# Gated two-layer block on one core: a new order in SP's DMA queue, gate and up products over three PSUM banks, and VectorE taking each unit one slot later

## What is computed

```
x = x + tanh(g_xattn[0]) * _L0_xattn_ref(_layernorm(x, axis=-1), ctx_1024, L0_xattn_W, L0_xattn_b)
x = x + tanh(g_ffn[0]) * _L0_ffn_ref(_layernorm(x, axis=-1), L0_ffn_w_up, L0_ffn_w_down)
x = x + tanh(g_xattn[1]) * _L1_xattn_ref(_layernorm(x, axis=-1), ctx_1024, mask, Wq, bq, Wkv, bkv, Wout, bout, 16)
x = x + tanh(g_ffn[1]) * _L1_ffn_ref(_layernorm(x, axis=-1), gate_w, up_w, down_w, s_in, s_in_down)
```

```
gate_out = nvfp4_linear(x, gate_w, s_in[0])
up_out = nvfp4_linear(x, up_w, s_in[0])
hidden = jax.nn.silu(gate_out) * up_out
return nvfp4_linear(hidden, down_w, s_in_down[0])
```

## Time and profile before

| | |
|---|---|
| median of 3 runs | 1825.38 us (1817.82 to 1830.28) |
| profiled execution | 1823.66 us, span of its trace 1821.9 us |
| mean granted TensorE clock | 0.892 of 2.4 GHz |
| busy share: PE, DVE, ACT, POOL | 75%, 78%, 38%, 13% |
| chain that ended last | issue 43%, DVE 26%, PE 18%, DMA 4%, SP's queue 4%, ACT 3% |

### The profile page before, as it was taken

The page is one execution under the profiler, slowest core; times in us unless marked ns, Lnnn a source line. Parts: engine busy times, 40 slices in busy tenths (PEclk is TensorE's granted clock), DMA queues, the critical chain, the costliest instruction groups (busy, mean ns, idle before and its releaser), DMA issues.

```text
span 1821.9 us, 24307 instructions
## 1 busy us (share of the span) xinstructions
PE 1371.2 (75%) x8120; PEld 705.4 (39%) x8120; DVE 1421.6 (78%) x2437; ACT 692.5 (38%) x2105; POOL 243.9 (13%) x197
## 2 busy tenths in 40 slices
PE   5044737799787978698778978797869886988663
PEld 4021315344453436344543345343634453434321
DVE  6988896878787687787787878768777778786695
ACT  2112206451455227441644146422734164425310
POOL 1102200131003200230013100320013001310000
PEclk9556868899889989999999989998999999999888
DMA  9175761042101420233004210142023300420012
GB/s 348 68 243 146 188 143 36 6 88 64 42 1 35 93 59 14 35 62 77 25 7 87 58 48 1 35 93 59 14 35 65 75 24 6 87 58 24 7 24 51
DMA packets 267433, 120.08 MB, mean 66 GB/s; under 512 B 244090, under 2 KB 244602, under 8 KB 265750
## 3 DMA queue, kind: packets, MB, share of 16 engines
q1 hardware_dynamic: 267286, 118.27, 26.5%
HBM read 49.04 MB, written 8.39 MB: 32 GB/s over the span
## 4 chain that ended last, share of the span: by engine, by line
issue 43%; DVE 26%; PE 18%; DMA 4%; SPq 4%; ACT 3%; POOL 2%; POOLq 0%; DVEq 0%; ACTq 0%
PE bank L1075 13%; PE bank L1164 5%; DVE amax L826 2%; DVE pair L835 2%; DVE hid L831 2%; SPq L314 2%; DVE th L868 2%; SPq L303 1%; DVE pair L850 1%; DMA region<-region 1%; ACT region L535 1%; DVE pair L843 1%; DMA hqt<-pair 1%; DVE sc L797 1%; DVE stats L686 1%
## 5 line engine op out<-in xcount | busy, mean ns | idle before, releaser
L1164 PE MATMUL bank<-w_dn,region 128*128 128x512 fp8e4 x1024 | 243.7, 386 | 40.0 <-DMA region<-region 40.0
L1075 PE MATMUL bank<-w_up,xt 128*128 128x512 fp8e4 x1024 | 248.6, 391 | 32.7 <-ACT region L499 17.4
L1075 PE MATMUL bank<-w_gate,xqt 128*128 128x512 bf16 x512 | 147.9, 416 | 122.2 <-DVE th L868 78.4
L508 ACT ACTIVATE th<-bank,half_cg 128x512 f32<-128x512 f32 x128 | 88.0, 687 | 350.2 <-PE bank L1075 350.2
L426 POOL TENSOR_TENSOR region<-g,region 128x512 f16<-128x512 f32 x128 | 178.9, 1402 | 300.9 <-ACT region L499 292.9
L868 DVE SCALAR_TENSOR_TENSOR th<-th,bank 128x512 f32<-128x512 f32 x128 | 87.6, 684 | 138.4 <-ACT th L508 138.3
L535 ACT ACTIVATE region<-bank,nm 128x77 f32<-128x77 f32 x512 | 160.0, 345 | 68.2 <-DVE nm L914 68.2
L1075 PE MATMUL bank<-w_down,hqt 128*128 128x512 bf16 x512 | 134.3, 422 | 56.9 <-DMA hqt<-pair 56.9
L496 ACT ACTIVATE g<-bank 128x512 f32<-128x512 f32 x128 | 76.4, 597 | 247.2 <-PE bank L1075 188.2
L1164 PEld LDWEIGHTS bank<-w_dn,region 128*128 128x128 f16 x1024 | 101.0, 99 | 167.4 <-issue 52.0
L1075 PEld LDWEIGHTS bank<-w_up,xt 128*128 128x128 f16 x1024 | 102.0, 101 | 163.5 <-issue 55.4
(11 more groups left out here) (206 smaller groups left out, 2473.6 us busy)
## 6 DMA issues: line engine op xcount, KB each, us to landing
xin<-in_x SPq DMA_DIRECT2D x16, 512.0 KB, 4.1
out_x<-x SPq DMA_DIRECT2D x16, 512.0 KB, 3.0
region<-in_w_up_t SPq DMA_DIRECT2D x1, 4096.0 KB, 12.9
hid<-in_gate_w SPq DMA_DIRECT2D x4, 1024.0 KB, 5.2
x<-in_gate_w SPq DMA_DIRECT2D x4, 1024.0 KB, 6.1
hid<-in_up_w SPq DMA_DIRECT2D x4, 1024.0 KB, 5.2
x<-in_up_w SPq DMA_DIRECT2D x4, 1024.0 KB, 5.8
hid<-in_down_w SPq DMA_DIRECT2D x4, 1024.0 KB, 4.9
```

Of the source, the lines that this page charges most:

```text
L508: eng.activation(th[:, u % 2, :], bank[4][:, :], ACT.Tanh, scale=half_cg[:, :]).then_inc(sg["th"], 1)
L1075: last = mm(out, lhs, rhs, start=(n == 0), stop=(n == len(pairs) - 1))
L1164: last = mm(bank[2 + t % 2][:, :], ht[i][:, t % 2, f, :], w_dn[:, f, :], start=(f == 0 and i == 0), stop=(f == KF - 1 and i == 1))
```

## The change

There are three edits.

1. `gu_bank(u, i)` deals the products of the units over banks 4, 5 and 6 in turn, in place of bank 4 for every gate and bank 5 for every up. A gate product now waits for hid of unit u-2, and an up product for hg of unit u-1. Unit 1's gate is the first to use bank 6, which phase A uses too, and so waits for `p3l`. ScalarE and VectorE read the banks by the same rule.
2. In phase B VectorE takes `hidden` of a unit in the slot behind TensorE's, and `QUANT_AT` moves by one slot: parts 0 to 2 to `TILE_AT`+5, parts 3 and 4 to `TILE_AT`+6. `POST_AT`, and with it the slots of down4 and out4, stays. In the tail VectorE's order is as it was.
3. SP's `turns` issues the transposes of hidden tiles 0 and 1 of stage 2 ahead of the first `turn_h`, and those of tiles 2 and 3 ahead of the second.

```diff
-QUANT_AT = {TILE_AT[t] + 4 + i: (t, q) for t in range(TILES) for i, q in enumerate(((0, 1, 2), (3, 4)))}
+QUANT_AT = {TILE_AT[t] + 5 + i: (t, q) for t in range(TILES) for i, q in enumerate(((0, 1, 2), (3, 4)))}
...
+        def gu_bank(u, i):
+
+            return 4 + (2 * u + i) % 3
...
                 if g1 is not None:
                     turn_ht(g1, 0)
+                    turn_ht(g1, 1)
                 turn_h(g, 0)
                 if g1 is not None:
-                    turn_ht(g1, 1)
                     turn_ht(g1, 2)
+                    turn_ht(g1, 3)
                 turn_h(g, 1)
-                if g1 is not None:
-                    turn_ht(g1, 3)
                 store(g, 0)
...
-                        if s in GU_AT:
-                            hidden(s4, GU_AT[s])
+                        if s - 1 in GU_AT:
+                            hidden(s4, GU_AT[s - 1])
...
-                for i, (w, read) in enumerate(((w_gate, "hg"), (w_gup, "hid"))):
-                    if u:
-                        want(pe, read, g, u)
+                for i, w in enumerate((w_gate, w_gup)):
+                    if i == 0 and u >= 2:
+                        want(pe, "hid", g, u - 1)
+                    if i == 1 and u:
+                        want(pe, "hg", g, u)
...
+                    if u == 1 and i == 0:
+                        want(pe, "p3l", g)
-                    last = product(bank[4 + i][:, :], [(xqt[:, t, k, :], w[:, k, ns]) for k in range(KD)])
+                    last = product(bank[gu_bank(u, i)][:, :], [(xqt[:, t, k, :], w[:, k, ns]) for k in range(KD)])
```

More of the change, by code:

```diff
@@ L507, in tanh4 @@
                     want(act, "hid", g, u - 1)
-                eng.activation(th[:, u % 2, :], bank[4][:, :], ACT.Tanh, scale=half_cg[:, :]).then_inc(sg["th"], 1)
+                eng.activation(th[:, u % 2, :], bank[gu_bank(u, 0)][:, :], ACT.Tanh, scale=half_cg[:, :]).then_inc(sg["th"], 1)
             def query(g, c):
@@ L867, in hidden @@
                 want(dve, "th", g, u + 1)
-                eng.scalar_tensor_tensor(th[:, u % 2, :], th[:, u % 2, :], 1.0, bank[4][:, :], ALU.add,
+                eng.scalar_tensor_tensor(th[:, u % 2, :], th[:, u % 2, :], 1.0, bank[gu_bank(u, 0)][:, :], ALU.add,
                                          ALU.mult).then_inc(sg["hg"], 1)
@@ L871, in hidden @@
                 want(dve, "gu", g, u + 1)
-                eng.tensor_tensor(buf[:, n * D:(n + 1) * D], th[:, u % 2, :], bank[5][:, :], ALU.mult).then_inc(sg["hid"], 1)
+                eng.tensor_tensor(buf[:, n * D:(n + 1) * D], th[:, u % 2, :], bank[gu_bank(u, 1)][:, :], ALU.mult).then_inc(sg["hid"], 1)
             def quant4(g, t, parts, buf=hid):
```

## The result

| | before | after |
|---|---|---|
| median | 1821.6 us (4 runs) | 1898.16 us (4 runs, 1892.76 to 1898.78) |
| ratio, 95% interval | | 1.0408 [1.037, 1.0446] |
| profiled execution, its span | 1823.66, 1821.9 us | 1898.78, 1897.0 us |
| mean granted TensorE clock | 0.892 | 0.868 of 2.4 GHz |
| down4 of tile 3 waits, in each of six phases | 4.21 to 4.86 us | 14.21 to 14.25 us |

The kernel is 4.1% slower, or 76.6 us. 1887 was forecast, with 1871 to 1902 as the range. A fourth run of the kernel before brought its median from 1825.38 to 1821.6 us.

A forecast was written before the change was run, and what follows sets the result against it. The prediction took VectorE and TensorE handing work to each other as the bound, with down4 of tile 3 waiting on VectorE's rounding. 60.0 (loop) + 3.8 (seventh phase) - 1.8 (tail) = +62.0 us gave 1887 us, range 1871 to 1902.

The forecast's parts named there:

- What bounds the kernel: VectorE and TensorE handing work over; down4 of tile 3 waits 4.86 us without slack, so lateness there delays the loop equally.
- the late rounding: Tile 3's rounding before down4: 10.0 us later in six loop phases, 60.0 us, plus 3.8 us in the seventh.
- The gates: Stage 4 gate and up products: waits move to up products, gains vanish by the first query; 0, bounds 1.3 us.
- The DMA order: SP's transposes reordered in the queue: saves a wait of about 0.6 us in some phases; priced at 0.
- The colder TensorE: Down4 of tile 3 after longer idleness: no dearer, 0 added; at most 1.7 us per phase, 12 us in all.
- The sum: Whole kernel: 60.0 + 3.8 - 1.8 = +62.0 us, so 1887 us on the scale of the median.
- The tail: After the seventh phase: gates run further ahead and waits for tanh fall away; -1.8 us, bounds 0 and -5.
- the fourth rival: Dearer: colder TensorE (+12 us) or a query 1.3 us later (+9 us), 1896 to 1908 us; chance 0.13.
- 1: Rival: rotating the gate banks returns the whole 78.4 us wait, tile 3's rounding having slack; 1747 us; chance 0.03.
- 2: Rival: gates running ahead start queries 7.8 us earlier per phase, cancelling the late rounding; 1832 us; chance 0.04.
- 3: Rival: first query starts 1.3 to 2.5 us sooner, shrinking VectorE's wait before it; 1870 us; chance 0.1.

The follow-up runs named there:

- e1: Changed kernel with only the rounding of tile 3 put back into slots 27 and 28; 1828.9 us, ratio 1.0037.
- e4: Changed kernel with norm1 moved from slot 29 to slot 30, behind parts 3 and 4 of tile 3's rounding; 1848.68 us, ratio 1.0152.
- e7: Kernel before with only `hidden` and the rounding one slot later, banks and SP's order as before; 1937.81 us, ratio 1.0608.
- e2: Kernel before with only the gate and up products dealt over banks 4, 5 and 6; 1819.78 us, ratio 0.9985.
- e3: Kernel before with only SP's new order of transposes; 1809.6 us, ratio 0.9944.
- e9: Changed kernel with `hidden` and the rounding back in their old slots, keeping three banks and SP's new order; 1819.1 us, ratio 0.997.
- e5: Changed kernel with 62 unread matmuls (34 in the seventh phase) before down4 of tile 3; 1876.9 us, ratio 1.0276.
- e8: e1 with the same unread matmuls as e6, before down4 of tile 3 and before unit 0's gate; 1815.0 us, ratio 0.9953.
- e11: e3 with 18 unread matmuls before down4 of tile 3 and none before unit 0's gate; 1809.16 us, ratio 0.9918.
- e6: e3 with 20 unread matmuls (18 in the seventh phase) before down4 of tile 3 and 22 before unit 0's gate; 1825.97 us, ratio 1.0008.
- e12: e3 with norm1 in slot 30 in place of 29; 1811.76 us, ratio 0.9932.
- e10: e3 with tile 3's five rounding parts all in slot 27; 1806.89 us, ratio 0.9901.

## Why the prediction came out as it did

**What bounds the kernel, and the late rounding.** Right. L853 was forecast 10.0 us later and is 10.0 us later; its parts were forecast at 2.55 and 7.41 us. The second is 7.41; the first shows as 2.98, of which 0.39 is only that VectorE is free sooner (at 881.89 - 2.98 = 878.91, 1.11 us behind the query's start, before 1.50). The wait before down4 was forecast at 14.8 us and is 14.22: SP's queue row

```profile
901.70 1.71 SPq L348 DMA_TRANSPOSE hqt<-pair  x1
```

stands 4.29 us ahead of down4's start at 905.99, where the kernel before needed 4.94. The working took that time as unchanged. In all, hqt cost 119.1 us of waiting (120 forecast), and 8.12 us in the seventh phase (8). Moving tile 3 alone (e1) gave back 69 us, norm1 alone (e4) 6.16 us of each wait.

**The gates.** Right in the end and not on the way there: the waits moved to the up products, and gate to query took 102.9 us against 102.6, where 0 with bounds of 1.3 was carried. But the gains in between, of 0.2, 0.7 and 1.9 us, did not come. On the mean of the six phases the up products of units 1, 5 and 13 start 0.2, 1.3 and 0.2 us later behind unit 0's gate than before. Unit 1 shows why. In all seven phases VectorE now has

```profile
781.71 1.15 POOL L429 TENSOR_TENSOR region<-g,region 128x512 f16<-128x512 f32 x1 [5.06 <-ACT region L502]
...
781.82 1.32 DVE L848 TENSOR_SCALAR pair<-pair 128x1024 uint16<-128x1024 uint16 x1
```

and the same row took 0.43 us in the phase that the prediction read. That the 0 came out is therefore in part luck: gains that were counted to vanish before the query had never been there. The change as a whole hides that its edits each do something here: by e7 and the changed kernel the late `hidden` costs 6 us per phase, and the third bank, perhaps with edit 3, gives them back. The page Perfetto Trace Analysis of the Trainium skill, section Matmuls, speaks for that rotation; by the runs it pays where the reader is a slot late (e7) and not where it is not (e2, 0.9985).

**The DMA order.** Priced at 0; alone it is worth 11.5 us (e3), on top of edit 1 only 3.4 (e9 against e2, each against its before). The step that failed is "what it saves is a wait of about 0.6 us": these waits went, but some 8 of the 11.5 us come with loop phases that take their shortest length. In the changed kernel, whose six row-to-gate stretches are all 30.2 us, nothing of this is to be seen.

**The colder TensorE.** This term, given as 0 with 12 us as the upper bound, was too small. It was taken as 0 since down4 behind 11.22 us of idleness had taken little longer (5.43 us) than behind 4.86 (5.09). In the changed kernel the stretch of that down4, in the form of the earlier trace rows, is

```profile
906.00:912.00 6.00, 6.00 (x15) 2.14 (x16) 0.00 (x0) 0.00 (x0) 0.00 (x0) 0.50 0.02 5
```

a clock of 0.50 throughout, where it averaged 0.70. The group of all down4 matmuls (total busy us, mean ns, idle us before them), after and then before:

```profile
L1078 PE MATMUL bank<-w_down,hqt 128*128 128x512 bf16 x512 | 145.8, 449 | 119.1 <-DMA hqt<-pair 119.1
```

```profile
L1075 PE MATMUL bank<-w_down,hqt 128*128 128x512 bf16 x512 | 134.3, 422 | 56.9 <-DMA hqt<-pair 56.9
```

has grown by 11.5 us. In the six loop phases down4 of tile 3 takes 6.57 us where it took 5.80 on the mean, 4.6 us in all and within the 1.7 us per phase that the bound allowed. The time at half clock has grown by 12 us per phase, but 11 of them lie between the first query and the end of down4, mostly where TensorE stands idle and the clock costs nothing. The rest of what was missed lies at slow stretches elsewhere, in the seventh phase and the tail. What misled is that the clock of down4 was inferred from the length of the one wait ahead of it: in the tail the same product took 5.43 us behind 11.22 us of idleness before, and takes 6.56 behind 10.10 now.

**The sum.** In the profiled executions the excess is 75.1 us against 62.0. The loop gave 62.1 (60.0 forecast): per phase 9.5 at the wait, 0.2 between gate and query, 0.6 from the start of down4 to the next such row. That this is so near is partly luck, since the earlier landing of hqt (0.65 us less in five of six phases) and the colder down4 (0.8 us more) cancel. From the eighth GpSimd row to down4 of tile 3 in the seventh phase it gave 10.1 where 3.8 was forecast; 4.4 of these lie ahead of unit 0's gate, where the row-to-gate stretch is 33.19 us and was 28.83 (TensorE is busy 22.05 us of it at a clock of 0.80, and was 17.53 at 0.95, with the same matmuls), 2.0 between the gate and the query, and 3.8 at the wait, as forecast. The tail gave 2.9, where -1.8 was forecast. The gain did come: the tail's first down4 starts 1.7 us sooner behind the seventh phase's. But the tail's four down4 products then take 24.2 us together where they took 17.7, the last of them

```profile
1885.60 6.56 PE L1078 MATMUL bank<-w_down,hqt 128*128 128x512 bf16 x16 [10.10 <-DMA hqt<-pair]
```

against the 5.43 us of the earlier trace rows. 2.1 + 6.3 + 4.7 = 13.1 us were missed, 11 of them behind the loop and with a slower clock beside them. That the clock is their cause is read from these stretches; e5 filled the waits of the seven phases, none in the tail, and so shows that a slow down4 costs, not that it makes up these 13 us. The measured 1898.16 us lies just above the forecast's own range (1877 to 1897) and in the range of the fourth rival (1896 to 1908), the dearer, colder TensorE with a chance of 0.13. The other rivals fell: 1 by e2, 2 and 3 by the first query, which starts no sooner in its phase (102.9 us behind the gate).

## What to carry to other kernels

Where engines work through fixed lists, price a moved step by everything it is put behind on its own engine, waits included, and ask of the last step of a phase first: here five instructions one slot later, with 7.4 us of other work and a 2.6 us wait let in ahead of them, cost 69 of 77 us. A further PSUM bank paid here beside a reader that is late by a slot and did nothing where the reader's engine was the bound. Filling TensorE's idle time is to be measured on the kernel at hand: it took off 24 us behind the 14 us wait (e5) and 17 us in short waits (e8 against e1), was worth nothing certain in one (e11) and cost 13 us in two (e6 against e3).

## What the runs showed of the hardware that was not expected

- **The lower clock decides more than small edits do.** The same 134 or 135 matmuls keep TensorE busy for 17.4 us at a granted clock of 0.95 and for 21.7 at 0.79, and the stretch between a GpSimd row and unit 0's gate takes 28.8 or 33.0 us with them. Which of the two a phase gets changes with edits elsewhere, and from phase to phase in the kernel before (28.8 to 33.1 us).
- **The loop settles on a few periods**, repeated to 0.4 us or better: 194.56 in e3, 197.97 in e9, 208.1 to 208.5 in the changed kernel, 215.0 in e7. A gain of 1 us in a phase can thus come out as nothing (e11) or as several (e3). The clock above and the GpSimd product below are two things that set these lengths; whether there are others was not tried.
- **GpSimd beside VectorE: who comes first counts.** An L834 that began inside a GpSimd product took 1.53 us in all seven cases of e6, and 0.69 alone. A later row of the same rounding (L845 before, L848 in the changed kernel) took 1.26 to 1.41 us where it began inside such a product, in all four cases before and all seven in the changed kernel, but 0.43 where it did not.
- **A transpose lands later beside a load of the program's own code.** From SP's row to down4's start the same transpose took 4.94 us in five loop phases before and 4.30 in the sixth, 4.29 to 4.33 in the changed kernel, and 5.55 to 6.14 with the filling of e6. norm1 is not the cause (e12: 4.96), and VectorE's work is not either: in the kernel before it is 4.08 us beside all six. What differs is one packet of 8 KB of another queue, some 3.7 us behind SP's row, here from 872.1 to 877.1 us in the kernel before:

```profile
q14 instruction: 1, 0.01, 0.4%
```

It is there in each of the five slower phases and not in the sixth, nor in any loop phase of the changed kernel; e1, e2, e3, e9, e11 and e12 divide in the same way, 4.94 to 4.97 with it and 4.29 to 4.32 without. The slowest landings, those of e6, have a 16 KB packet of the same kind as well. In e10 the packet is there and the time is 4.37, so it costs less there. That the packet is the cause is argued from these traces; no run moved it alone.
